# Value products of the first attention as float32 column tiles, four heads at a time

## The reference

```
s = q @ k.T / 4 + slope * (i - j), -inf above the diagonal
p = softmax(s);  o = p @ v;  out = concat(o) @ Wp.T
```

## Time and profile before

| | |
|---|---|
| median of 3 runs | 2409.69 us (2409.5 to 2412.82) |
| profiled execution | 2411.58 us, its span 2409.8 us |
| mean granted TensorE clock | 0.930 |
| PE, DVE, ACT, POOL busy over the whole span | 83%, 75%, 66%, 46% |
| first attention | from about 27 to 683 us |

### The profile page before, as it was taken

How to read it: one execution, slowest core, us unless ns; L and a number is a source line. 1 busy time by engine, 2 the same in 40 slices (tenths; PEclk the granted TensorE clock), 3 DMA queues, 4 the chain that set the end, 5 groups by cost and what they waited for, 6 DMA issues and landing times. The chain is left out here.

```text
span 2409.8 us, 59672 instructions
## 1 busy us (share of the span) xinstructions
PE 2005.5 (83%) x19526; PEld 1471.0 (61%) x19527; DVE 1807.8 (75%) x3763; ACT 1594.6 (66%) x3182; POOL 1112.8 (46%) x1290
## 2 busy tenths in 40 slices
PE   2998888889880899468799999999899999739999
PEld 1676666667670566245476667676666767625665
DVE  3897898879984344458678796969787886589997
ACT  1998898889972344257668686868777787534443
POOL 4546454545305000388756564746556474032222
PEclk8999999999965999779999999999999999869999
DMA  7000000000024233102100000000000000100000
GB/s 231 2 2 3 3 2 2 3 3 2 2 79 151 84 93 87 22 9 28 27 2 3 2 2 2 2 3 2 3 2 3 1 2 2 37 0 11 17 17 25
DMA packets 53185, 58.58 MB, mean 24 GB/s; under 512 B 7120, under 2 KB 47216, under 8 KB 52896
## 3 DMA queue, kind: packets, MB, share of 16 engines
q1 hardware_dynamic: 46240, 45.00, 6.1%
q0 software_dynamic: 6656, 9.85, 1.9%
HBM read 36.22 MB, written 18.61 MB: 23 GB/s over the span
## 5 line engine op out<-in xcount | busy, mean ns | idle before, releaser
L529 DVE TENSOR_REDUCE neg_max_sb<-a_bank 128x1 f32<-128x128 f32 (+3 forms) x1024 | 471.3, 481 | 185.9 <-PE a_bank L286 183.6
L432 ACT ACTIVATE prob_sb<-a_bank,neg_max_sb 128x128 f32<-128x128 f32 (+3 forms) x1024 | 533.7, 555 | 89.4 <-DVE neg_max_sb L529 85.0
L440 ACT ACTIVATE p_hi_sb<-a_bank 128x384 f16<-128x384 f32 (+1 forms) x768 | 424.4, 553 | 142.3 <-PE a_bank L295 140.9
L536 DVE TENSOR_TENSOR p_lo_sb<-a_bank,p_hi_sb 128x384 f16<-128x384 f32 (+1 forms) x768 | 453.9, 592 | 55.0 <-ACT p_hi_sb L440 52.5
L295 PE MATMUL a_bank<-ident_f_sb,prob_sb 128*128 128x128 f32 x2560 | 418.6, 279 | 0.6 <-ACT prob_sb L432 0.6
L451 ACT ACTIVATE stack_sb<-a_bank 102x1024 bf16<-102x1024 bf16 (+2 forms) x384 | 346.3, 902 | 43.6 <-PE a_bank L340 41.9
L369 PE MATMUL a_bank<-w_in_sb,xnT_sb 128*128 128x512 f16 x1152 | 290.1, 390 | 29.2 <-DVE t_buf_sb L577 20.9
L295 PEld LDWEIGHTS a_bank<-ident_f_sb,prob_sb 128*128 128x128 f32 x2560 | 274.9, 144 | 53.5 <-issue 1.4
L286 PE MATMUL a_bank<-mask_sb,ident_b_sb 128*128 128x128 bf16 x1024 | 223.1, 224 | 0.0
L705 POOL TENSOR_TENSOR rope_w_sb<-t_buf_sb,sin_sb 128x256 f32<-128x256 f32 x128 | 124.9, 975 | 170.0 <-DVE t_buf_sb L577 168.1
L315 PE MATMUL a_bank<-v_stage_sb,p_hi_sb 128*128 128x65 f16 x1280 | 159.7, 194 | 36.7 <-DVE y_sb L548 35.8
(11 more groups left out here) (231 smaller groups left out, 4897.6 us busy)
## 6 DMA issues: line engine op xcount, KB each, us to landing
sorted_rows<-zeros_sb SPq DMA_DIRECT2D x1, 4992.0 KB, 23.3
x_in_sb<-sorted_rows SPq DMA_DIRECT2D x39, 128.0 KB, 2.1
sorted_results<-y_moe_sb SPq DMA_DIRECT2D x39, 128.0 KB, 1.7
x_sb_sb<-L_attn_x SPq DMA_DIRECT2D x8, 512.0 KB, 10.6
w_raw_sb<-L_ffn_gate_bank SPq DMA_DIRECT2D x8, 512.0 KB, 4.2
w_raw_sb<-L_ffn_up_bank SPq DMA_DIRECT2D x8, 512.0 KB, 5.3
w_raw_sb<-L_ffn_down_bank SPq DMA_DIRECT2D x8, 512.0 KB, 6.7
out<-x_sb_sb SPq DMA_DIRECT2D x32, 128.0 KB, 1.7
```

What stands on the lines that cost most here:

```text
L432: last = act.activation(prob[g][:, off:off + L], S[(3 * h + g) % 2][:, off:off + L], ACT.Exp, bias=neg_max[:, i:i + 1])
L440: act.activation(p_hi[g][:, h % 2, :], PT[g][:, 0:GROUP_COLS[g]], ACT.Copy).then_inc(s_hi, 1)
L529: last = dve.tensor_reduce(neg_max[:, i:i + 1], S[(3 * h + g) % 2][:, off:off + L], AX.X, ALU.max, negate=True)
L536: dve.tensor_tensor(p_lo[g][:, h % 2, :], PT[g][:, 0:GROUP_COLS[g]], p_hi[g][:, h % 2, :], ALU.subtract).then_inc(s_lo, 1)
```

## The change

The first attention gets a function of its own, `attention0`; the second keeps `attention`. In it:

- the probabilities stay float32: `hi` and `lo` are gone. ACT copies the first transposed group (512 columns) of a head from PSUM to `probT`, DVE the other two (512 and 256 columns). The ten transposes of a head are dealt as 4, 4 and 2, by key tile;
- `v_stage` is float32, 32 columns a head (16 values, a one, zeros), written by DVE straight from the projection's bank; POOL no longer spreads values, and `parts` and `rest` hold q and k only;
- the product is turned round: v (128 x 32) is stationary, the transposed probabilities move. Four heads j take the array's columns 32j to 32j+31 (`tile_position=(0, 32 * j)`) and write 32 partitions each of one bank. One key tile kt of the four heads (512, 384, 256, 128 columns) is done in each of four slots that follow each other, from slot 12c + 17 on for quad c;
- ACT then copies the bank (`take_out`), PE transposes it back (`oT`), DVE inverts the row sums and scales (`y`);
- ACT copies the stack of the even heads, DVE that of the odd ones;
- the slots of all side work move (`AT0`).

```diff
--- before.py
+++ after.py
@@ -47,6 +47,8 @@
 
 
 
+LAGS0 = (4, 1, 8)
+AT0 = ((9, 11, 13, 14), (20, 22, 25, 26), (32, 35, 37, 40), 22, 24, (63, 64, 66, 67))
 LAGS = ((2, 2, 3, 4, 0, 1), (2, 2, 3, 4, 0, 1))
 
 
@@ -761,6 +763,475 @@
         run(pool, prologue, slot, [chain], besides=aside and aside[2])
+def attention0(block, x_sb, stats, consts, w, sem, sb, banks, lags, at):
+    LAG_T, LAG_EV, LAG_PV = lags
+    LAG_WA, LAG_WV = 0, 1
+    AT_1, AT_XT, AT_0, AT_OT, AT_YT, AT_PROJ = at
+    DH, HC = DH0, 8
+    CHUNKS, QUADS = HEADS // HC, HEADS // 4
+    PIECES = 4
+    VW = 32
+    KT_COLS = [(QT - kt) * P for kt in range(QT)]
+    T_GROUPS = (((0, 0), (1, 0), (2, 0), (3, 0)), ((1, 1), (2, 1), (3, 1), (3, 3)), ((2, 2), (3, 2)))
+    KT_AT = {0: 0, 1: 512, 3: 896, 2: 1024}
+    T_AT = (0, 512, 1024, 1280)
+    IN_GROUP = {i: (g, sum((j + 1) * P for j in tiles if j < i)) for g, tiles in enumerate(GROUP_TILES) for i in tiles}
...
+    v_stage = sb("v_stage0", [P, 2, QT, 8, VW], F32)
...
+    prob = [sb(f"prob0_{g}", [P, 2, n], F32) for g, n in enumerate(GROUP_COLS)]
+    probT = sb("probT0", [P, 2, 4, T_AT[3]], F32)
...
+    def work(k, last):
+        out = []
+        nxt = [] if last else [1]
+        h, r = divmod(k, 3)
+        if 0 <= k < GROUPS and r == 0:
+            out += [("stack", 0, h + 1)] if h + 1 < HEADS else [("stack", 1, 0) for _ in nxt]
+        out += [("piece", 0, 1, p) for p, at_ in enumerate(AT_1) if at_ == k]
+        for _ in nxt:
+            out += [("xT", 1, j) for j, at_ in enumerate(AT_XT) if at_ == k]
+            out += [("piece", 1, 0, p) for p, at_ in enumerate(AT_0) if at_ == k]
+        out += [("oT", 0, c) for c in range(QUADS) if k == 12 * c + AT_OT]
+        out += [("yT", 0, c) for c in range(CHUNKS) if k == 24 * c + 12 + AT_YT]
+        out += [("proj", 0, i) for i, at_ in enumerate(AT_PROJ) if at_ == k]
+        return out
+    assert AT_PROJ[-1] - GROUPS < 12 + AT_YT
+    TAIL = AT_PROJ[-1] + 1 + LAG_WV
+    FILLS_W = HEADS + 2 * PIECES + QT + QUADS + CHUNKS + QT
...
+        def transpose_probs(b, h, r):
+            H = b * HEADS + h
+            if r == 0:
+                wait(pe, s_exp, 3 * (H + 1))
+                wait(pe, s_pta, H)
+            else:
+                wait(pe, s_ptv, 2 * H - 2 + r)
+            for n, (i, kt) in enumerate(T_GROUPS[r]):
+                g, off = IN_GROUP[i]
+                last = pe.transpose(PT[r][:, n * P:(n + 1) * P],
+                                    prob[g][:, h % 2, off + kt * P:off + (kt + 1) * P], ident_f[:, :])
+            last.then_inc(s_pt, 1)
+        def pv(b, c, part):
+            Q = b * QUADS + c
+            if part == 0:
+                wait(pe, s_oT, Q)
+                wait(pe, s_taken, b * 2 * PIECES + (c // 2 + 1) * PIECES)
+                wait(pe, s_pta, 4 * (Q + 1))
+                wait(pe, s_ptv, 8 * (Q + 1))
+            for kt in (part,):
+                for j in range(4):
+                    last = pe.matmul(ob[32 * j:32 * j + VW, kt * P:T], v_stage[:, c // 2, kt, 4 * (c % 2) + j, :],
+                                     probT[:, c % 2, j, KT_AT[kt]:KT_AT[kt] + KT_COLS[kt]],
+                                     start=kt == 0, stop=kt == QT - 1, tile_position=(0, 32 * j))
+            if part == QT - 1:
+                last.then_inc(s_pv, 1)
...
+            elif kind == "oT":
+                c, = a
+                wait(pe, s_oT, b * QUADS + c + 1)
+                for i in range(QT):
+                    last = pe.transpose(out[:, i * P:(i + 1) * P], oT[:, i * P:(i + 1) * P], ident_f[:, :])
+                taken[bank] = (s_y, QUADS, off, c + 1)
...
+        def slot(cur, off, k, last):
+            b = cur + off
+            if k < GROUPS:
+                scores(b, k // 3, k % 3)
+            if 0 <= k - LAG_T < GROUPS:
+                transpose_probs(b, (k - LAG_T) // 3, (k - LAG_T) % 3)
+            for kind, ahead, *a in work(k, last):
+                fill(cur, off + ahead, kind, *a)
+            c, part = divmod(k - 9 - LAG_PV, 12)
+            if 0 <= c < QUADS and part < QT:
+                pv(b, c, part)
...
+        def exp(b, h, g):
+            wait(act, s_max, b * GROUPS + 3 * h + g + 1)
+            if g == 0:
+                wait(act, s_pt, 3 * (b * HEADS + h - 1))
+            off = 0
+            for i in GROUP_TILES[g]:
+                L = (i + 1) * P
+                last = act.activation(prob[g][:, h % 2, off:off + L], S[(3 * h + g) % 2][:, off:off + L], ACT.Exp, bias=neg_max[:, i:i + 1])
+                off += L
+            last.then_inc(s_exp, 1)
+        def take_probs(b, h):
+            H = b * HEADS + h
+            wait(act, s_pt, 3 * H + 1)
+            wait(act, s_pv, b * QUADS + h // 4 - 1)
+            act.activation(probT[:, (h // 4) % 2, h % 4, T_AT[0]:T_AT[1]], PT[0][:, :], ACT.Copy).then_inc(s_pta, 1)
+        def take_out(b, c):
+            Q = b * QUADS + c
+            wait(act, s_pv, Q + 1)
+            wait(act, s_y, Q)
+            act.activation(oT[:, :], ob[:, :], ACT.Copy).then_inc(s_oT, 1)
+        def take(kind, b, *a):
+            bank, n = work_banks.next(kind)
+            if kind == "stack":
+                h, = a
+                if h % 2 == 0:
+                    wait(act, s_st, b * HEADS + h + 1)
+                    wait(act, s_scores, 3 * (b * HEADS + h - 1))
+                    act.activation(stack[0:K0, 0, :], W[bank][:, :].bitcast(BF16)[0:K0, :], ACT.Copy).then_inc(s_stev[0], 1)
...
+        def slot(cur, off, k, last):
+            b = cur + off
+            h, r = divmod(k - LAG_T - LAG_EV, 3)
+            if r == 0 and 0 <= h < HEADS:
+                take_probs(b, h)
+            if k < GROUPS:
+                exp(b, k // 3, k % 3)
+            c, r = divmod(k - 13 - LAG_PV, 12)
+            if r == 0 and 0 <= c < QUADS:
+                take_out(b, c)
+            for kind, ahead, *a in work(k - LAG_WA, last):
+                take(kind, b + ahead, *a)
...
+        def take_probs(b, h, r):
+            H = b * HEADS + h
+            wait(dve, s_pt, 3 * H + r + 1)
+            wait(dve, s_pv, b * QUADS + h // 4 - 1)
+            dve.tensor_copy(probT[:, (h // 4) % 2, h % 4, T_AT[r]:T_AT[r + 1]],
+                            PT[r][:, 0:T_AT[r + 1] - T_AT[r]]).then_inc(s_ptv, 1)
+        def take(kind, b, *a):
+            bank, n = work_banks.next(kind)
+            if kind == "stack":
+                h, = a
+                if h % 2:
+                    wait(dve, s_st, b * HEADS + h + 1)
+                    wait(dve, s_scores, 3 * (b * HEADS + h - 1))
+                    dve.tensor_copy(stack[0:K0, 1, :], W[bank][:, :].bitcast(BF16)[0:K0, :]).then_inc(s_stev[1], 1)
+            elif kind == "piece":
+                half, p = a
+                m = b * 2 * PIECES + half * PIECES + p
+                wait(dve, s_fill, n)
+                wait(dve, s_piece, m - 1)
+                dve.wait_ge(s_ph, m + 1)
+                dve.tensor_tensor(rest[:, p % 2, :, :], W[bank][:, 0:256].rearrange("p (h d) -> p h d", d=DH),
+                                  parts[:, p % 2, :, 0, :], ALU.subtract)
+                wait(dve, s_pv, (b - 1) * QUADS + 2 * half + 2)
+                dve.tensor_copy(v_stage[:, half, p, :, 0:DH],
+                                W[bank][:, 256:384].rearrange("p (h d) -> p h d", d=DH)).then_inc(s_taken, 1)
+            elif kind == "oT":
+                c, = a
+                Q = b * QUADS + c
+                o = W[bank][:, :].rearrange("p (i j d) -> p i j d", j=4, d=VW)
+                wait(dve, s_fill, n)
+                dve.reciprocal(rsum[:, :].rearrange("p (i j) -> p i j", j=4), o[:, :, :, DH]).then_inc(s_rs, 1)
+                wait(dve, s_rs, Q + 1)
+                wait(dve, s_yT, b * CHUNKS + c // 2 - 1)
+                half = (c % 2) * 4 * DH
+                dve.tensor_tensor(y[:, (c // 2) % 2, :, half:half + 4 * DH].rearrange("p i (j d) -> p i j d", d=DH),
+                                  o[:, :, :, 0:DH],
+                                  rsum[:, :].rearrange("p (i j) -> p i j", j=4).unsqueeze(3).to_broadcast([P, QT, 4, DH]),
+                                  ALU.mult).then_inc(s_y, 1)
...
+        def slot(cur, off, k, last):
+            b = cur + off
+            if k < GROUPS:
+                row_max(b, k // 3, k % 3)
+            if k + 1 in AT_XT and not last:
+                normalize(b + 1, AT_XT.index(k + 1))
+            for kind, ahead, *a in work(k - LAG_WV, last):
+                take(kind, b + ahead, *a)
+            h, r = divmod(k - LAG_T - LAG_EV, 3)
+            if r and 0 <= h < HEADS:
+                take_probs(b, h, r)
...
+        def take(b, half, p):
+            m = b * 2 * PIECES + half * PIECES + p
+            wait(pool, s_taken, m + 1)
+            r, q = rest[:, p % 2, :, :], parts[:, p % 2, :, :, :]
+            own(first_copy(q[:, :, 1, :], r))
+            own(pool.tensor_tensor(q[:, :, 2, :], r, q[:, :, 1, :], ALU.subtract))
```

(14 more changed lines are left out.)

236 lines of the change are left out of this document (added).

## The result

The changed kernel takes 2458.06 us (median of 4 runs, 2454.41 to 2462.58) against 2411.26 for the one before in the same session (4 runs): ratio 1.0193, interval 1.0171 to 1.0215. It is 47 us slower where 69 were forecast, inside the range and with the forecast sign. The reason given for it was wrong in its largest term, and other losses, not priced, took its place.

A forecast was written before the change was run, and what follows sets the result against it. ACT was taken to bound free slots, PE those with a piece. Per batch -15.4 + 16.3 + 2.65 + 2.4 + 2.5 = +8.5; eight batches +68, ends +1: +69 us, 2480; range 2365 to 2560.

The forecast's parts named there:

- The rule of slots: First attention: a batch sums each slot's slowest engine; tested on the old kernel, 77.5 us against 78.6.
- pieces: Projection pieces of the next batch: seven outside product slots, one inside, 8.5 us against 6.1, +2.4 a batch.
- The relief of ACT and DVE: First attention, work a head: ACT falls from 3.86 to 2.63 us, DVE comes to 2.84.
- free slots: Slots without side work: 1.29 us becomes 0.97, with DVE ending last; -15.4 us a batch.
- The products at 5t: Product slots: column tiles overlap only in pairs, t being one record; 5.33 us a quad, +16.3 a batch; 45%.
- 2t: Product slots: all four heads' float32 products run together, two records' time each, 2.13 us a quad.
- The change of mode: Product slots: two changes between full-width matmuls and column tiles, each 0 to 0.16 us; half taken, 2.65 a batch.
- the drain: Array running dry at mode changes, 0 to 5.3 us a batch; total +50 us with none, +92 with all.
- Full overlap: Rival for the product slots: four heads run together, -30 us, 2382, with 2360 to 2403; chance 33%.
- oT: New transposes of the products, with DVE's reciprocal and multiplication behind them: +2.5 us a batch where DVE sets the slot.
- The prologue's gain: Before the loop: POOL loses copies where four pieces follow each other, -5 us once.
- the tail: Kernel's end: last quad's products, one more copy, transposes and lag against the old product and reduction, +6 us once.

The follow-up runs named there:

- e10: e8 with three quads' product slots a batch reordered, transposes split two and two around the first products, one mode change more: 2392.57 us against 2387.59.
- e2: The changed kernel with each head's product issued twice, the two next to each other: 2528.42 us.
- e8: Changed kernel with products in one slot a quad, ACT taking their bank three slots earlier, all stacks on ACT, side work dealt out anew: 2387.59 us.
- e4: The changed kernel with the oT transposes and yT one slot later: 2429.11 us, ratio 1.0085 to the kernel before the change.

## Why the prediction was right, and where it was wrong

- *The rule of slots* (a batch is the sum of each slot's slowest engine) held where one engine fills the slot: pieces without a wait take 2.0 us, product slots what PE needs. It fails where a chain over several engines sets the slot: the 3.03 us of slot 37, the 4.4 behind the jump. The relief of ACT and DVE was there, but free slots take 1.06 on average, not 0.97, so that less than the 15.4 us a batch arrived.
- *The products at 5t* was the step that failed. "If that order holds among column tiles too" did not hold: 2t, 2.13 us a quad. The four slots take 6.18 us where free ones of 0.97 take 3.88: 2.3 a quad, 9.2 a batch with the changes of mode in it, against 16.3 + 2.65.
- *The change of mode* was bounded by 0 and 0.33 a slot, taken as 0.16, and measures 0.24 (0.29 in slots 17 and 41 of e10). That agrees with the drain that the Trainium skill names in TensorEngine Tiling (Array Packing), Key Properties; its cost is less than the sum, since free slots cover part of it. The Trainium skill's other rule, strict program order of starts (TensorE: Matmul & The Clock Gate, Part 3), did not hold across column tiles in e2; its measured speed-up of three tiles did point the right way.
- *Full overlap*, the rival that was found true, had been given 2382. It lacked a term: waits of side work, 62 us in eight batches where there had been 10, 6.5 a batch more, of which the forecast had 2.5 under "oT", as DVE's time. Of the moved stack copy the forecast named what DVE would spend on it (0.60) and not what waits for the bank that it releases.
- The books per batch: -15.4 (free slots, as forecast) + 9.2 (products, modes) + 2.4 (pieces, as forecast) + 6.5 (side work's waits) + 1.7 (sixteen oT transposes of 0.11) = +4.4, against 85.9 - 79.1 = +6.8 measured in the four batches from the same slot (79.1: four batches of the kernel before, from 205.4 to 521.7, each with a stop at the jump). 2.4 a batch stays unexplained. Two things bear on it. Free slots at 1.06 in place of 0.97 would add 48 x 0.09 = 4.3, an estimate that assumes all slots fall short alike. And the jump did not stay as it was: a pass costs 3.9 us now (85.9 less 82.0), before about 5.6 (79.1 less 73.5, the loop's first batch without the stop at its end), 1.7 less.
- The prologue's gain was right: the first scores start 4.5 us earlier (55.3 for 59.8 us), 5 were forecast. From the last slot on, the kernel is 2.0 us longer, where 6 were forecast for the tail.
- So sign and size came out, by two errors that nearly cancel: 9.8 us a batch too much for the products, and some 8 too little for waits, oT and what stays unexplained. That they cancel is luck.
- Slips in the forecast that change nothing: DVE is busy 85% in the earlier trace rows, not 86, and 69 us without the drain or with all of it are +48 and +90, not +50 and +92.

## What to carry to other kernels

When two engines share a few work banks in strict turn, a copy moved to another engine must be priced by when it releases its bank, not only by how long it takes. Look for a fill that wants that bank in the next slot: the move of one copy cost 33 us here, some 8 of them at the loop's jump, and nothing away from the jump where the fills stood apart. A loop's jump stops an engine for a while (PE 3.9 us before, DVE 3.0 after), and whether others wait for it can hang on the work that stands just before it: about 20 of the 29 us of a later oT lay there. So read a batch with and one without a jump before you say where a gain comes from; a total that meets the expectation does not show its reason. A saving on an engine counts only in slots that this engine sets; three changes of mode less a quad gave nothing, since 0.55 of their 0.72 us had covered time in which PE would have been idle. And a relief of the bounding engine needs the schedule dealt out again: the same arithmetic was 1.9% slower than before with the first schedule and 0.9% faster with the one of e8.

## What the runs showed of the hardware

Four float32 products of 128 x 32 weights in four column tiles run at the same time: four records of 617 ns start within 0.02 us, and 512 columns for four heads take 0.85 us beside 0.24 for going over and back. A product that waits for its own tile does not hold up products for other tiles, with up to four records of one tile in a row (e2: 2.69 us for 2.67).

At the loop's jump DVE starts its next instruction 3.0 us after its last one, five times in the changed kernel (15.0 us), and PE, idle for 3.5 us behind it, then works at a granted clock of 0.50 (301.67 to 304.50), the lower of its two levels. In e4, where nobody waits for the jump, the batch behind it has a granted clock of 1.00.
